# Issuing a group's four key tiles of the product with V as two pairs instead of four single jobs

## The reference, cut to what matters

```python
def reference(x, ctx_1024, g_xattn, g_ffn, ...):       # x: 16 x 512 x 256
    x = x + tanh(g_xattn[0]) * xattn(layernorm(x), ctx_1024, Wq, Wk, Wv, Wo, bo)
    x = x + tanh(g_ffn[0]) * ffn(layernorm(x), gate_w, w_gate, w_up, w_down)

def xattn(x, context, Wq, Wk, Wv, Wo, bo):             # 16 heads of 16 columns
    q, k, v = x @ Wq.T, context @ Wk.T, context @ Wv.T
    scores = einsum('bhqd,bhkd->bhqk', q, k) * 16**-0.5
    probs = softmax(where(causal, scores, -inf))
    return einsum('bhqk,bhkd->bhqd', probs, v) @ Wo.T + bo
```

## Time and profile before

| | |
|---|---|
| Median of the runs | 2008.08 us (3 runs, 2006.38 to 2014.46) |
| The profiled execution | 2008.71 us; its span, first to last instruction, 2006.9 us |
| TensorE busy | 1847.0 us (92%), mean granted clock 0.973 |
| VectorE busy | 1122.4 us (56%) |
| ScalarE, GpSimd busy | 898.1 us (45%), 709.5 us (35%) |

### The profile page before, as it was taken

The page is one execution under the profiler, slowest core; times in us unless marked ns, Lnnn a source line. Parts: engine busy times, 40 slices in busy tenths (PEclk is TensorE's granted clock), DMA queues, the critical chain, the costliest instruction groups (busy, mean ns, idle before and its releaser), DMA issues.

```text
span 2006.9 us, 41634 instructions
## 1 busy us (share of the span) xinstructions
PE 1847.0 (92%) x13800; PEld 1091.3 (54%) x13800; DVE 1122.4 (56%) x2745; ACT 898.1 (45%) x1716; POOL 709.5 (35%) x636
## 2 busy tenths in 40 slices
PE   3799999999999999992599999999999999999997
PEld 1455555555555555551256556565555656566565
DVE  3667787788887778766543443434333433434332
ACT  1355555555556555562243343433333333433332
POOL 4234444444444444223324233332424233342322
PEclk9799999999999999996799999999999999999999
DMA  4655565555555655526456454664545646444322
GB/s 128 147 143 144 162 166 154 155 149 161 156 161 161 167 158 163 132 82 154 132 103 125 81 98 85 115 122 85 99 81 95 122 74 120 94 73 90 58 28 26
DMA packets 378619, 238.32 MB, mean 119 GB/s; under 512 B 260600, under 2 KB 360064, under 8 KB 378496
## 3 DMA queue, kind: packets, MB, share of 16 engines
q1 hardware_dynamic: 353920, 203.14, 41.0%
q0 software_dynamic: 24576, 33.57, 10.6%
HBM read 118.63 MB, written 58.72 MB: 88 GB/s over the span
## 4 chain that ended last, share of the span: by engine, by line
PE 48%; DVE 2%; DMA 2%; issue 1%; POOL 0%; ACT 0%; DVEq 0%; POOLq 0%
PE bank L1037 11%; PE bank L1038 10%; PE bank L1039 10%; PE bank L1055 5%; PE bank L1053 5%; PE bank L1054 5%; DMA out<-y,row_now 1%; DVE top_at L1106 1%; DVE work L1109 1%; DVE top L1104 1%; POOL out L997 0%; DVE h L1144 0%; DMA tokT<-rows 0%; ACT y L1091 0%; POOL rows L989 0%
## 5 line engine op out<-in xcount | busy, mean ns | idle before, releaser
L558 ACT ACTIVATE prob<-bank 128x512 f32<-128x512 f32 x640 | 372.5, 597 | 221.6 <-PE bank L448 210.4
L997 POOL DMA_INDIRECT out<-y,row_now x128 | 201.6, 1575 | 661.4 <-ACT y L1091 637.1
L1144 DVE TENSOR_TENSOR h<-bank,silu 128x512 f32<-128x512 f32 x256 | 176.3, 689 | 341.4 <-PE bank L1039 340.4
L645 DVE CUSTOM_DVE_ANT_0 masked<-bank,causal 128x384 f32<-128x384 f32 (+1 forms) x512 | 299.3, 617 | 44.9 <-PE bank L428 44.1
L1083 ACT ACTIVATE h<-h 128x512 bf16<-128x512 f32 x256 | 161.1, 629 | 348.7 <-DVE h L1144 348.7
L428 PE MATMUL bank<-ks,qs 96*128 96x128 bf16 (+3 forms) x1024 | 277.8, 307 | 29.9 <-DMA ks<-k_parts 25.8
L1053 PE MATMUL bank<-downT,h 128*128 128x256 bf16 x1024 | 279.1, 273 | 0.0
L1054 PE MATMUL bank<-downT,h 128*128 128x256 bf16 x1024 | 279.1, 273 | 0.0
L1055 PE MATMUL bank<-downT,h 128*128 128x256 bf16 x1024 | 279.1, 273 | 0.0
L1147 DVE TENSOR_TENSOR h<-h 128x512 bf16<-128x512 f32 x256 | 177.2, 692 | 179.5 <-ACT h L1083 179.5
L446 PE MATMUL bank<-qs,ks 98*128 98x512 bf16 (+3 forms) x1024 | 268.4, 301 | 3.0 <-DMA qs<-m_sb 2.2
(11 more groups left out here) (144 smaller groups left out, 2784.0 us busy)
## 6 DMA issues: line engine op xcount, KB each, us to landing
qs<-q_parts SPq DMA_DIRECT2D x384, 64.0 KB, 2.7
ks<-k_parts SPq DMA_DIRECT2D x384, 64.0 KB, 2.7
q_parts<-q_sb SPq DMA_DIRECT2D x32, 384.0 KB, 3.1
k_parts<-k_sb SPq DMA_DIRECT2D x32, 384.0 KB, 3.2
x_t<-in_x SPq DMA_DIRECT2D x16, 512.0 KB, 4.1
ctx_t<-in_ctx SPq DMA_DIRECT2D x16, 512.0 KB, 4.9
res_t<-in_x SPq DMA_DIRECT2D x16, 512.0 KB, 5.6
out<-x SPq DMA_DIRECT2D x16, 512.0 KB, 3.0
```

Of the source, the lines that this page charges most:

```text
L558: nc.scalar.activation(prob[:, gr % 2, h0:h0 + nh, POFF[tiles[0]]:POFF[tiles[0]] + w], sc_bank[SC_BANK[k]][:, 0:nh * w].rearrange("p (h w) ...
L645: nc.vector.tensor_tensor_reduce(masked[:, k % 2, 0:w], max_bank[max_at(gr, k)][:, 0:w], causal[:, T - w:T], 1.0, LOWEST, ALU.add, ALU.max ...
L997: nc.gpsimd.indirect_dma_start(out_rows, bass.IndirectOffsetOnAxis(ap=row_now[:, par, CHUNK * c + s:CHUNK * c + s + 1], axis=0), y[:, c % ...
```

## The change

The four `pv` jobs of a group, which stood at four different steps, are now issued two by two: tiles 0 and 1 at one step, tiles 2 and 3 at another. Within a pair nothing stands between the jobs on TensorE. `pv+` moves by a step for three of the groups. Everything else keeps its step; `steps` still yields the same pieces, and the instructions of a `pv` job are the same.

| group | tiles 0, 1, 2, 3 before | pairs after | `pv+` before, after |
|---|---|---|---|
| 0 | 3:4, 3:6, 3:8, 3:10 | 3:5, 3:8 | 3:10, 3:10 |
| 1 | 0:0, 0:1, 0:3, 0:5 | 0:2, 0:5 | 0:6, 0:7 |
| 2 | 1:3, 1:5, 1:7, 1:9 | 1:4, 1:7 | 1:10, 1:9 |
| 3 | 1:10, 2:1, 2:4, 2:5 | 2:1, 2:4 | 2:7, 2:6 |

```diff
--- before.py
+++ after.py
@@ -64,6 +64,11 @@
 PALL = sum(PWIDTH)
 
 
+def half_pv(b, gr, half):
+
+    return [("pv", b, gr, 2 * half), ("pv", b, gr, 2 * half + 1)]
+
+
 def starts_job(p):
 
     return p[0] in JOBS_A_BATCH and (len(p) < 4 or p[3] == 0)
@@ -77,36 +82,36 @@
 
 
     extra = {
-        0: {0: [("pv", b - 1, 1, 0), ("ln1+", b + 1, 0)],
-            1: [("yt", b - 1, 0), ("pv", b - 1, 1, 1), ("xsplit", b + 1, 0), ("ln1+", b + 1, 1)],
-            2: [("yt+", b - 1, 0), ("yb", b - 2, 1), ("xsplit", b + 1, 1)],
-            3: [("pv", b - 1, 1, 2), ("mrow", b - 1, 3), ("yb+", b - 2, 1)],
+        0: {0: [("ln1+", b + 1, 0)],
+            1: [("yt", b - 1, 0), ("xsplit", b + 1, 0), ("ln1+", b + 1, 1)],
+            2: [("yt+", b - 1, 0)] + half_pv(b - 1, 1, 0) + [("yb", b - 2, 1), ("xsplit", b + 1, 1)],
+            3: [("mrow", b - 1, 3), ("yb+", b - 2, 1)],
             4: [("mt+", b - 1, 3), ("mt", b - 1, 3)],
-            5: [("pv", b - 1, 1, 3), ("o+", b - 2, 0), ("o", b - 2, 0, 0), ("o", b - 2, 0, 1), ("xturn", b + 1)],
-            6: [("pv+", b - 1, 1), ("csplit", b + 1, 0), ("csplit", b + 1, 1)],
-            7: [("o", b - 2, 1, 0), ("o", b - 2, 1, 1), ("o+", b - 2, 1)],
+            5: half_pv(b - 1, 1, 1) + [("o+", b - 2, 0), ("o", b - 2, 0, 0), ("o", b - 2, 0, 1), ("xturn", b + 1)],
+            6: [("csplit", b + 1, 0), ("csplit", b + 1, 1)],
+            7: [("pv+", b - 1, 1), ("o", b - 2, 1, 0), ("o", b - 2, 1, 1), ("o+", b - 2, 1)],
             10: [("yt", b - 1, 1), ("stack", b, 2), ("cturn", b + 1)]},
         1: {1: [("mt", b, 0)], 2: [("yt+", b - 1, 1)],
-            3: [("pv", b - 1, 2, 0), ("mt+", b, 0), ("ln2", b - 2, 0)],
-            4: [("q", b + 1, 0, 0), ("q", b + 1, 0, 1), ("q+", b + 1, 0)],
-            5: [("pv", b - 1, 2, 1), ("ln2", b - 2, 1)],
+            3: [("mt+", b, 0), ("ln2", b - 2, 0)],
+            4: half_pv(b - 1, 2, 0) + [("q", b + 1, 0, 0), ("q", b + 1, 0, 1), ("q+", b + 1, 0)],
+            5: [("ln2", b - 2, 1)],
             6: [("q", b + 1, 1, 0), ("q", b + 1, 1, 1), ("q+", b + 1, 1)],
-            7: [("pv", b - 1, 2, 2)], 8: [("mrow", b, 0)],
-            9: [("pv", b - 1, 2, 3), ("xs", b - 2), ("ln2+", b - 2, 1)],
-            10: [("pv+", b - 1, 2), ("ln2+", b - 2, 0), ("pv", b - 1, 3, 0)]},
-        2: {1: [("stack", b, 3), ("qstore", b + 1), ("mt", b, 1), ("mt+", b, 1), ("pv", b - 1, 3, 1)],
+            7: half_pv(b - 1, 2, 1), 8: [("mrow", b, 0)],
+            9: [("pv+", b - 1, 2), ("xs", b - 2), ("ln2+", b - 2, 1)],
+            10: [("ln2+", b - 2, 0)]},
+        2: {1: [("stack", b, 3), ("qstore", b + 1), ("mt", b, 1), ("mt+", b, 1)] + half_pv(b - 1, 3, 0),
             2: [("yt+", b - 1, 2), ("mrow", b, 1)],
             3: [("yt", b - 1, 2), ("yb", b - 1, 0), ("yb+", b - 1, 0), ("k+", b + 1, 0)],
-            4: [("k", b + 1, 0, 0), ("k", b + 1, 0, 1), ("pv", b - 1, 3, 2)],
-            5: [("k", b + 1, 1, 0), ("pv", b - 1, 3, 3), ("load", b + 2), ("k+", b + 1, 1), ("k", b + 1, 1, 1)],
-            7: [("pv+", b - 1, 3), ("vaug", b)], 8: [("xt+", b - 2, 0), ("res", b - 1), ("xt", b - 2, 0)],
+            4: [("k", b + 1, 0, 0), ("k", b + 1, 0, 1)] + half_pv(b - 1, 3, 1),
+            5: [("k", b + 1, 1, 0), ("load", b + 2), ("k+", b + 1, 1), ("k", b + 1, 1, 1)],
+            6: [("pv+", b - 1, 3)], 7: [("vaug", b)], 8: [("xt+", b - 2, 0), ("res", b - 1), ("xt", b - 2, 0)],
             9: [("xt", b - 2, 1)], 10: [("xt+", b - 2, 1)]},
         3: {0: [("kstore", b + 1)], 1: [("mt", b, 2)],
             2: [("mrow", b, 2), ("mt+", b, 2), ("yt", b - 1, 3), ("yt+", b - 1, 3)], 3: [("ll+", b - 2)],
-            4: [("pv", b, 0, 0), ("ll", b - 2), ("v", b + 1, 0, 0), ("v", b + 1, 0, 1), ("v+", b + 1, 0)],
-            5: [("ln1", b + 2, 0)], 6: [("stack", b + 1, 0), ("lt", b - 2), ("lt+", b - 2), ("pv", b, 0, 1)],
-            8: [("v+", b + 1, 1), ("v", b + 1, 1, 0), ("pv", b, 0, 2), ("v", b + 1, 1, 1)],
-            9: [("stack", b + 1, 1)], 10: [("pv+", b, 0), ("pv", b, 0, 3), ("save", b - 2), ("ln1", b + 2, 1)]},
+            4: [("ll", b - 2), ("v", b + 1, 0, 0), ("v", b + 1, 0, 1), ("v+", b + 1, 0)],
+            5: half_pv(b, 0, 0) + [("ln1", b + 2, 0)], 6: [("stack", b + 1, 0), ("lt", b - 2), ("lt+", b - 2)],
+            8: [("v+", b + 1, 1), ("v", b + 1, 1, 0)] + half_pv(b, 0, 1) + [("v", b + 1, 1, 1)],
+            9: [("stack", b + 1, 1)], 10: [("pv+", b, 0), ("save", b - 2), ("ln1", b + 2, 1)]},
     }
     for g in range(GROUPS):
         sc = (b, g - 2) if g >= 2 else (b - 1, g + 2)
```

## The result

| | before | after |
|---|---|---|
| Median of 7 runs each | 2009.04 us (2006.38 to 2014.46) | 2021.42 us (2017.85 to 2023.49) |
| Ratio | | 1.006, 95% interval 1.0047 to 1.0073 |
| The profiled execution, its span | 2008.71, 2006.9 us | 2021.35, 2019.5 us |
| TensorE busy | 1847.0 us | 1834.4 us |
| `experts` begins on TensorE at | 926.41 us | 939.27 us |

A forecast was written before the change was run, and what follows sets the result against it. TensorE's queue was taken to set the time, except in two stretches set by VectorE's chains. Twelve bodies at +0.8 us gave +9.6, the ends -5: +4.6, so 2008.7 becomes 2013 us; range for 8 in 10: 1997 to 2023.

The forecast's parts named there:

- Pairs: `pv` on TensorE: tiles 0 and 1 together take 1.64 us, 2 and 3 0.79, each 0.24 less with lead.
- The stretches: Windows from `max` 3:9 to `mt` 0:4, `q` 1:4, `mt` 2:1, `max` 3:9: 8.9, 11.9, 9.3, 23.4 us.
- Both VectorE chains: VectorE sets two stretches: `max` 3:9 to `yq` (8.22 us), and `q`'s end to `mt` 2:1 (9.34 us).
- The waits: TensorE's `mt` on `yq` 1.5 to 1.8 us a batch; new waits on VectorE's maxima; none for `pv_read`.
- the second chain gives way: Rival, 1:4 to 2:1: VectorE has room, stretch takes 7.7 us, total 1993; chance 0.2 including the first chain giving too.
- GpSimd's contention: Rival: GpSimd's splitting of q slows VectorE's four `ln2+` operations, 1.0 us a batch, total 2025; chance 0.15 with smaller misjudged queues.
- the pair isn't cheaper: Rival: a pair costs the sum less 0.09, 0.85 us more a batch, total 2024; chance 0.03.
- The ends: Bodies 1, 14, 15, 16, slots into them, body 2 and drain: TensorE's gain comes through, -5 us, range -8 to -2.
- together -5: Sum for the ends: -1.3 each in bodies 1 and 15, -0.5 each into 1, 15, 16, -1 for 2, 14, drain.

The follow-up runs named there:

- the split kernel: Changed kernel with each of the eight pairs taken apart by one neighbouring piece, same work in each stretch: 2038.53 us, 1.0144 of before.
- the control: Kernel before, single jobs kept, second halves of `ln1` moved to 3:5 and of `ln2` to 1:3: 2010.59 us, 0.9999 of before.
- the kernel with three holes in a row: Changed kernel with second halves of `ln1`, `ln2` early, group 2's first pair behind `q`, group 0's at 3:4 before `ll`: 2019.56 us, 1.0051.

## Why the prediction was right in kind and short in size

**Pairs.** Forecast 1.64 and 0.79 from the drain; measured 1.64 and 0.79 in the loop, and 0.23 a pair by the split kernel. Right. That TensorE's busy time falls by 0.85 a batch and not by 1.7 doesn't contradict it: a row lasts until its results are out, so in front of each new hole a job's tail counts as busy. That this is all of the difference isn't shown; the worth of the pairs, 1.4 to 1.6 us a batch, stands in the control.

**The stretches.** Forecast 8.9, 11.9, 9.3, 23.4; measured 8.92, 11.94, 9.27, 23.39. The batch was forecast at 53.55 and took 53.52. Both VectorE chains were shown by shortening them: with the second half of `ln1` out of it the first stretch falls by 1.6, with that of `ln2` out of it the third by 1.06, and no other stretch falls with either.

**The waits.** `mt` on `yq` up to 1.5, on average 1.3 (forecast 1.5 to 1.8), on the maximum at 2:1 0.3 (0.5), `max` on VectorE's up to 0.5 (0.4 to 0.6), `pv_read` none. Right.

**The rivals.** That the second chain gives way is out: the third stretch stayed at 9.27. GpSimd's contention would have lengthened the same chain: out. That the pair isn't cheaper: out by the split kernel.

**The ends: here it failed.** The prediction has one term, "together -5", for everything outside the regular loop, and took its sign from the missing layer norms; it had named these ends as the place to look if the windows held and the total didn't. Its parts, set against the trace of before (the -1 for bodies 2, 14 and the drain in equal shares):

| | forecast | measured | the same kernel again |
|---|---|---|---|
| up to 3:9 of body 0 | 0 | +1.9 | -0.4 |
| body 1 | -1.8 | -0.7 | -1.8 |
| bodies 2 and 3 | +1.3 | 0.0 | 0.0 |
| body 4 | +0.8 | +4.3 | +3.2 |
| bodies 5 to 13 | +7.2 | +6.9 | +6.9 |
| body 14 to the end | -2.9 | +0.4 | +1.1 |
| sum, up to `experts` | +4.6 | +12.9 | +9.1 |

The start and body 1 scatter. Two steps are wrong in both traces. One is the bodies from 14 on, where TensorE's gain was expected to come through because a chain is missing, and the next wait takes much of it. These are the first piece of body 15 and the drain's first pair:

```profile
851.63 0.23 PE L433 MATMUL bank<-ks,qs 96*128 96x128 bf16 x1 [2.13 <-DMA ks<-k_parts]
...
914.62 1.71 PE L466 MATMUL bank<-prob,v_aug 128*32 128x512 f32 x16 [1.42 <-ACT yT L571]
```

Before, TensorE waited 1.34 us for k's DMA there, and the drain 1.00 for `yT`: 1.2 us of the gain are these two. In the second trace the wait for k is only 1.18, and body 15 does gain 1.2 us of the 1.8 that were forecast for it; but the drain's wait is 1.42 again, and the clock falls once more behind it. In both, body 14 costs 0.5, and what follows body 15 gains nothing (+0.2 and +1.8). The other step is body 4. The prediction asked of the queues only whether a moved piece is waited for sooner, and looked at batches of the steady loop. In the first trip of the loop k's store, its stack and TensorE were already tight (9.39 us for the stretch in the kernel before, against 8.93), and a store issued 3.0 us behind a 512 KB load, and not 4.2, was 1.4 us longer on its way. With the falling clock behind it this made 3.2 to 4.3 us, about a third of the loss up to `experts` in either trace. With that load out of the way the ratio is 1.0027, beside the 1.0023 that the forecast amounts to; since only 1.5 to 2.6 us of this can be put down to the load, the closeness is in part luck.

**Carried to the range.** 2021.4 lies in 1997 to 2023, but at its edge, and just above the forecast's own 2006 to 2021. The +0.6% falls under "slower by more than 0.5%", which had 0.26 against 0.55 for "same", and neither of the rivals that stood for it came true: the one-off price of the loop's first trip was in none of the cases.

## What to carry to other kernels

Grouping jobs to save switches on the busiest engine pays only where that engine sets the stretch; cut a period into stretches by who ends last, and book each moved piece by what leaves a covered stretch and what enters an uncovered one, before counting the saving. A hole is not room by itself: if the chain that makes it begins with the engine's own results, work put ahead of them lengthens the chain. The regular loop of this change could be forecast to 0.05 us from one trace; where the moved pieces shifted the head of a chain, the same walk missed by 1.4 to 1.9 us a batch. The first trip and the drain can't be lumped into one term: walk their DMA queue too.

## What the runs showed of the hardware

**The clock falls behind holes, and not in every batch.** In bodies 5 to 13 of the kernel before, holes are at most 0.7 us and the granted clock stays at 1.00. With holes of 1.5 us or more, or several close together, it went to 0.50 for 3.4 us in bodies 5 to 14 of five kernels, in some batches and not in others with the same rows; each such fall cost 1.6 us, and in the kernel with three holes in a row it came in six batches of ten. In other kernels with the same hole of 1.5 us, the changed one among them, it came in none of these bodies, and one wait of 2.56 us passed without it. A saving on TensorE that ends in a hole can thus cost more than nothing. What separates a batch with a fall from one without isn't settled here.

**A job in 32-column parts between full-width jobs pays for standing alone.** It is 0.23 to 0.24 us, by both comparisons. Going from bfloat16 to float32 isn't what costs: four full-width float32 transpositions take 0.44 us between bfloat16 jobs and 0.53 ahead of a `pv` job, which is the 0.09 again that the prediction found ahead of `pv`:

```profile
428.79 0.60 PE L474 MATMUL bank<-ident,yT 128*128 128x128 f32 x4
429.23 0.22 PE L428 MATMUL bank<-ks,qs 96*128 96x128 bf16 x1
...
418.36 0.60 PE L474 MATMUL bank<-ident,yT 128*128 128x128 f32 x4
418.89 0.85 PE L461 MATMUL bank<-prob,v_aug 128*32 128x384 f32 x8
```

The Trainium skill ("TensorEngine Tiling (Array Packing)", Key properties) says that a change of the tiling mode drains TensorE; the sign of these numbers agrees. That the drain is what they measure isn't shown.

**A store queued near behind a large load lands later.** In body 3, the two stores of 384 KB landed in 6.2 us (median) when issued 2.2 us behind a 512 KB load, in 4.7 to 5.0 at 2.7 to 3.3 us, and in 3.5 to 4.1 at 3.9 to 4.3 us. With the load moved behind them it was 3.2.
